# The adapter's transposes and outputs issued between the maxima of the first two units; the value weights in arrays of their own; the first attention loads at the adapter's beginning

## What is computed

```python
qkv = jnp.einsum('btc,oc->bto', x, w_attn)
q, k, v = jnp.split(qkv, 3, axis=-1)          # then 32 heads of 16, q and k rotated
scores = jnp.einsum('bhqd,bhkd->bhqk', q, k) / jnp.sqrt(hd)
attn = jax.nn.softmax(jnp.where(causal, scores, -jnp.inf), axis=-1)
y = jnp.einsum('bhqk,bhkd->bhqd', attn, v)
...
aqkv = jnp.einsum('btc,oc->bto', adapter_wte[None], w_attn)
_, ak, av = jnp.split(aqkv, 3, axis=-1)
ascores = jnp.einsum('bhqd,xhkd->bhqk', q, ak) / jnp.sqrt(C)
ascores = gating[0] * jax.nn.softmax(ascores, axis=-1)
y = y + jnp.einsum('bhqk,xhkd->bhqd', ascores, av)
return jnp.einsum('btc,oc->bto', y, w_proj)
```

## Time and profile before

| | us |
|---|---|
| median of three runs | 1001.11 (1001.0 to 1004.68) |
| the profiled execution: its own time | 1001.68 |
| its span, first to last instruction | 1000.0 |
| adapter stage on PE, first score to the last V product | 89.66 to 126.92 |
| the rest of the adapter on PE and the change of stage | 126.92 to 136.93 |
| first maxima, up to the first scores (L911) | 136.93 to 163.87 |

### The profile page before, as it was taken

The page is one execution under the profiler, slowest core; times in us unless marked ns, Lnnn a source line. Parts: engine busy times, 40 slices in busy tenths (PEclk is TensorE's granted clock), DMA queues, the critical chain, the costliest instruction groups (busy, mean ns, idle before and its releaser), DMA issues. The chain is left out here.

```text
span 1000.0 us, 15159 instructions
## 1 busy us (share of the span) xinstructions
PE 914.7 (91%) x5334; PEld 505.8 (51%) x5334; DVE 648.2 (65%) x1151; ACT 519.6 (52%) x1160; POOL 286.4 (29%) x527
## 2 busy tenths in 40 slices
PE   6897989999999998989689799999999889799997
PEld 4575853434444432865366334343444338577766
DVE  5954447877778760874736678787787418454464
ACT  4441322776767666222734147677776652367630
POOL 2666041223223221024247123222223221013200
PEclk9997985999999999987889789999999999899999
DMA  9331061122212110300014401011110010412001
GB/s 325 97 111 63 1 150 29 52 55 54 66 50 64 38 50 1 106 1 0 1 61 126 116 22 41 26 37 39 40 26 3 2 42 1 151 68 72 14 32 53
DMA packets 50029, 57.14 MB, mean 57 GB/s; under 512 B 8928, under 2 KB 39712, under 8 KB 49952
## 3 DMA queue, kind: packets, MB, share of 16 engines
q1 hardware_dynamic: 48320, 55.75, 18.5%
q10 hardware_dynamic: 1632, 0.39, 0.2%
HBM read 43.41 MB, written 12.32 MB: 56 GB/s over the span
## 5 line engine op out<-in xcount | busy, mean ns | idle before, releaser
L1026 DVE TENSOR_REDUCE mx<-psum 128x1 f32<-128x512 f32 (+3 forms) x640 | 370.8, 631 | 116.4 <-PE psum L891 72.3
L886 PE MATMUL psum<-arena_s 96*128 96x512 bf16 (+3 forms) x768 | 228.2, 352 | 10.3 <-PEq L246 5.9
L972 ACT ACTIVATE arena_p<-psum 128x512 f32<-128x512 f32 (+1 forms) x384 | 185.0, 591 | 93.1 <-PE psum L911 61.4
L911 PE MATMUL psum<-arena_s 99*128 99x512 bf16 (+3 forms) x768 | 204.3, 335 | 8.4 <-ACT arena_p L972 3.3
L972 ACT ACTIVATE arena_x<-psum 128x128 f32<-128x128 f32 (+2 forms) x384 | 134.0, 439 | 87.7 <-PE psum L911 64.8
L886 PEld LDWEIGHTS psum<-arena_s 96*128 96x128 bf16 x768 | 71.5, 100 | 125.5 <-DVE mx L1026 70.2
L911 PEld LDWEIGHTS psum<-arena_s 99*128 99x128 bf16 x768 | 66.9, 98 | 100.0 <-ACT arena_p L972 34.0
L1077 POOL TENSOR_SCALAR_AFFINE_SELECT arena_p<-arena_p 128x256 f32<-128x256 f32 x128 | 50.9, 408 | 204.1 <-ACT arena_p L972 204.1
L891 PE MATMUL psum<-maskb,ident_b 128*128 128x128 bf16 (+1 forms) x384 | 97.5, 254 | 0.0
L261 PE MATMUL psum<-x_h,w 128*128 128x512 f32 x224 | 86.5, 449 | 11.6 <-DVE w L497 8.4
L929 PE MATMUL psum<-arena_p,v_grp 128*32 128x512 f32 (+1 forms) x768 | 90.7, 592 | 0.0
(11 more groups left out here) (210 smaller groups left out, 1186.1 us busy)
## 6 DMA issues: line engine op xcount, KB each, us to landing
arena_s<-q_parts SPq DMA_DIRECT2D x32, 192.0 KB, 2.9
arena_s<-k_parts SPq DMA_DIRECT2D x96, 64.0 KB, 2.3
ff_raw<-in_w_in SPq DMA_DIRECT2D x11, 512.0 KB, 3.5
arena_s<-q_parts SPq DMA_DIRECT2D x32, 128.0 KB, 2.9
arena_w<-in_w SPq DMA_DIRECT2D x12, 256.0 KB, 6.5
q_parts<-arena_p SPq DMA_DIRECT2D x24, 128.0 KB
ff_wd_raw<-in_w_down SPq DMA_DIRECT2D x1, 2560.0 KB, 11.5
k_parts<-arena_p SPq DMA_DIRECT2D x18, 128.0 KB
```

Of the source, the lines that this page charges most:

```text
L886: last = pe.matmul(psum[:, bank, width * n:width * n + width], q_st[0:KS, b % NS, 512 * r + P * i:512 * r + P * i + P], k_st[0:KS, g % NK, ...
L911: pe.matmul(psum[:, 2 * (n % 2) + t, o:512], k_st[0:KM, g % NK, at:at + P], q_st[0:KM, u % NS, 512 * r + o:512 * r + 512], start=True, sto ...
L972: act.activation(pr[n % NP_RING][:, t, o:512], psum[:, 2 * (n % 2) + t, o:512], ACT.Exp, scale=scale).then_inc(exp_ready, 1)
L1026: dve.tensor_reduce(mx[:, b % 2, kc, col:col + 4 * len(heads) - 3:4], src, AX, ALU.max)\
```

## The change

Three edits go together.

First, the turns T and the outputs y leave the adapter stage. There remain scores 0, V0, V1, scores 1 and V2 to V7, with ACT's copies of V. In `attention` of the first layer, PE issues T of tile n after entry 5n of the first maxima and y of tile n after entry 5n + 3, in the PSUM banks 0 to 3. ACT copies them there (in the changed kernel L987 and L990), and its `load_max(0)` comes after the sixth tile. The first scores wait until all eight tiles are copied.

Second, the value columns of the weights get arrays of their own, `wv0`, behind the query and key columns in the same part of `arena_s`.

Third, SP issues `load_first` at the adapter's beginning, once the stores of the stage before have landed; it no longer waits for V7.

```diff
-        w0_hl = [at(f"w0_{n}", M_S + 24576 * n, [P, KC, 3 * C], F32R) for n in range(2)]
+        w0_hl = [at(f"w0_{n}", M_S + 24576 * n, [P, KC, 2 * C], F32R) for n in range(2)]
+        wv0_hl = [at(f"wv0_{n}", M_S + 24576 * n + 16384, [P, KC, C], F32R) for n in range(2)]
...
-    order = [("scores", 0), ("V", 0), ("V", 1), ("scores", 1)]
...
+    order = [("scores", 0), ("V", 0), ("V", 1), ("scores", 1)] + [("V", n) for n in range(2, NT)]
...
         def _(sp):
-
-            sp.wait_ge(turn_ready, turns.index(("V", NT - 1)) + 1)
             stacked.wait_stored(sp)
             stacked.load_first(sp)
...
+                if ad and n == 0:
+                    pe.wait_ge(turn_taken, NT)
+                    pe.wait_ge(y_copied, NT)
...
-            maxima(0, 0)
+            def adapter_turn(n):
+
+                if n >= 2:
+                    pe.wait_ge(turn_taken, n - 1)
+                for t in range(KC):
+                    last = pe.transpose(psum[0:AW, n % 2, P * t:P * t + P],
...
+            def adapter_values(n):
+
+                pe.wait_ge(turn_taken, n + 1)
+                if n >= 2:
+                    pe.wait_ge(y_copied, n - 1)
+                for t in range(KC):
+                    last = pe.matmul(psum[:, 2 + n % 2, P * t:P * t + P], ad["pT"][:, n % 2, t, :],
...
+            for e in range(issued_by(0, 0)):
+                b = next(x for x in range(NU + 1) if issued < first_entry[x + 1])
+                entry(issued, b, lists[b][issued - first_entry[b]])
+                issued += 1
+                tile, step = divmod(e, 5)
+                if ad and tile < NT and step == 0:
+                    adapter_turn(tile)
+                if ad and tile < NT and step == 3:
+                    adapter_values(tile)
...
-            load_max(0)
+            for n in range(NT if ad else 0):
+                act.wait_ge(turn_ready, n + 1)
...
+                act.wait_ge(y_ready, n + 1)
+                act.copy(ad["y"][:, n, :], psum[:, 2 + n % 2, :]).then_inc(y_copied, 1)
+                if n == NT - 3:
+                    load_max(0)
```

More of the change, by code:

```diff
@@ L189, in build @@
             arena_f=arena_f, ident=ident, ident_b=ident_b, maskb=maskb, psum=psum, v_grp=v_grp,
-            w_hl=w0_hl, x_hl=x0_hl, q_parts=q_parts[0], k_parts=k_parts[0], ones=ones, eps=eps,
+            w_hl=w0_hl, wv_hl=wv0_hl, x_hl=x0_hl, q_parts=q_parts[0], k_parts=k_parts[0], ones=ones, eps=eps,
             small_loads=[
@@ L199, in build @@
         wo = [view(arena_f, 8192 * n, [KC, C]) for n in range(2)]
-        adapter(nc, d, ad, x_loaded, x_tok, v_tok, w0_hl, x0_hl, arena_o, ident, gating, psum, stacked,
+        adapter(nc, d, ad, x_loaded, x_tok, v_tok, wv0_hl, x0_hl, arena_o, ident, gating, psum, stacked,
                 wo[0], wo_hl[0])
         attention(nc, 0, att, stacked, arena_o, arena_p, arena_x, v_tok, v_grp, ident_b, maskb, psum,
-                  (x_tok[:, :, :], d["x"].rearrange("(t p) c -> p t c", p=P), x_loaded))
+                  (x_tok[:, :, :], d["x"].rearrange("(t p) c -> p t c", p=P), x_loaded), ad, ident)
         w1_raw = view(v_tok[:, :, :].rearrange("p t c -> p (t c)"), 0, [KC, C + 2 * P])
@@ L317, in cut_of @@
         kind, k, n0 = piece
+        if kind == "w" and n0 == 2 * C:
+            return [w[:, k, n0:n0 + 512], *[a[:, k, :] for a in m["wv_hl"]]]
         return [a[:, k, n0:n0 + 512] for a in ((x_raw, xh, xl) if kind == "x" else (w, wh, wl))]
@@ L565, in _, with adapter @@
                     .then_inc(res_ready, 1)
-def adapter(nc, d, ad, x_loaded, x_tok, v_tok, w_hl, x_hl, arena_o, ident, gating, psum, stacked,
+def adapter(nc, d, ad, x_loaded, x_tok, v_tok, wv_hl, x_hl, arena_o, ident, gating, psum, stacked,
             wo_raw, wo_hl):
@@ L577, in adapter @@
     prob = [view(arena_o, 16384 + 5120 * n, [HT, H * ADP]) for n in range(2)]
-    pT = view(arena_o, 16384 + 10240, [2, KC, P], parts=AW)
-    mx, y_ad = ad["mx"], ad["y"]
-    order = [("scores", 0), ("V", 0), ("V", 1), ("scores", 1)]
[L583 to L591, removed]
+    mx = ad["mx"]
+    ad["prob"] = prob
+    ad["pT"] = view(arena_o, 16384 + 10240, [2, KC, P], parts=AW)
+    order = [("scores", 0), ("V", 0), ("V", 1), ("scores", 1)] + [("V", n) for n in range(2, NT)]
     def heads(a):
@@ L599, in adapter @@
                                                     ("scores_ready", "shifted", "exped", "prob_ready"))
-        turn_ready, turn_taken, y_ready, y_copied = (ph.sem(n) for n in
-                                                     ("turn_ready", "turn_taken", "y_ready", "y_copied"))
+        turn_ready, turn_taken = ph.sem("turn_ready"), ph.sem("turn_taken")
         chain_s = ph.sem("chain")
@@ L628, in _ @@
                     continue
[L629 to L651, removed]
+                if n >= 2:
+                    pe.wait_ge(turn_taken, n - 1)
+                products(pe, psum[:, 4 + n % 2, :],
+                         [lambda k, a=a: a[:, k, P * n:P * n + P] for a in x_hl],
+                         [lambda k, a=a: a[:, k, :] for a in wv_hl]).then_inc(turn_ready, 1)
         @block.scalar
@@ L655, in _ @@
             for what, n in order:
[L656 to L671, removed]
+                if what == "V":
+                    act.wait_ge(turn_ready, n + 1)
+                    if n == 2:
+                        stacked.wait_stored(act)
+                    act.copy(v_tok[:, n, :], psum[:, 4 + n % 2, :]).then_inc(turn_taken, 1)
                 if what == "V" and n in (0, 2):
@@ L761, in attention @@
 def attention(nc, layer, phase, stacked, arena_o, arena_p, arena_x, v_tok, v_grp, ident_b, maskb,
-              psum, x_load=None):
+              psum, x_load=None, ad=None, ident=None):
     q_st, k_st, q_loaded, k_loaded, kr = stacked.q, stacked.k, stacked.q_loaded, stacked.k_loaded, stacked.kr
@@ L837, in attention @@
         o_copied, vg_ready = ph.sem("o_copied"), ph.sem("vg_ready")
+        if ad:
+            turn_ready, turn_taken, y_ready, y_copied = (ph.sem(n) for n in
+                                                         ("turn_ready", "turn_taken", "y_ready", "y_copied"))
         block = ph.block()
@@ L942, in maxima @@
                     issued += 1
-            maxima(0, 0)
+            def adapter_turn(n):
+                if n >= 2:
+                    pe.wait_ge(turn_taken, n - 1)
+                for t in range(KC):
+                    last = pe.transpose(psum[0:AW, n % 2, P * t:P * t + P],
+                                        ad["prob"][n // (NT // 2)][:, n % (NT // 2), AW * t:AW * t + AW],
+                                        ident[:, :])
+                last.then_inc(turn_ready, 1)
+            def adapter_values(n):
+                pe.wait_ge(turn_taken, n + 1)
+                if n >= 2:
+                    pe.wait_ge(y_copied, n - 1)
+                for t in range(KC):
+                    last = pe.matmul(psum[:, 2 + n % 2, P * t:P * t + P], ad["pT"][:, n % 2, t, :],
+                                     ad["av_bd"][:, t, :], start=True, stop=True)
+                last.then_inc(y_ready, 1)
+            for e in range(issued_by(0, 0)):
[7 more added lines that the diff above has]
+                    adapter_values(tile)
             for u, kt in blocks[0:2]:
@@ L984, in load_max @@
                     .then_inc(max_loaded[u % NS], 16)
-            load_max(0)
+            for n in range(NT if ad else 0):
+                act.wait_ge(turn_ready, n + 1)
+                if n >= 2:
+                    act.wait_ge(y_ready, n - 1)
+                act.copy(ad["pT"][:, n % 2, :, :], psum[0:AW, n % 2, :].rearrange(
+                    "p (t q) -> p t q", q=P)).then_inc(turn_taken, 1)
+                act.wait_ge(y_ready, n + 1)
+                act.copy(ad["y"][:, n, :], psum[:, 2 + n % 2, :]).then_inc(y_copied, 1)
+                if n == NT - 3:
+                    load_max(0)
+            if not ad:
+                load_max(0)
             for u in range(NU):
```

## The result

The changed kernel takes 990.54 us (median of 4 runs, 989.28 to 992.53) against 1001.06 of the kernel before: a ratio of 0.9885, interval 0.9856 to 0.9914. Two further sets of runs gave 0.9859 (0.981 to 0.9907) and 0.9869 (0.9834 to 0.9903). It is faster by 1.15 to 1.41% in the three sets, each interval clear of 1; 990.8 was forecast.

What follows compares the result with a forecast made beforehand. PE bounds the adapter until V7, then SP's issues end it; DVE bounds the first maxima. 11.5 us saved less 1.2 gives 10.3: 1001.68 to 991.4, less 0.57 for the median, 990.8; range 987.6 to 995.5.

Steps and rivals of the forecast that it cites:

- The stage's end: Adapter stage: ends 11.5 us earlier, 2.84 from moved turns and outputs, 8.63 from ending with ACT's copy of V7.
- the 8.6 us of tail: Adapter's end: 8.63 us from ACT's copy of V7 to SP's last issue, removable only with early loads.
- Hidden behind DVE at full clock: First maxima: at 2.4 GHz PE's entries, T and y need 21.7 us, below DVE's 24.8, so they cost nothing.
- The sum's 2.5 of 2.7 us for five entries: First maxima: per five entries with their T and y, PE needs 2.5 us against DVE's 2.7.
- Friction and spells: First maxima: DVE waits behind unit 0's T plus zero to two low-clock spells, 0 to 4.2 us together, taken as 1.2.
- priced `load_max(0)` at nothing: First maxima: its 1.34 us issue on ACT delays T6's copy, needed by y6 only 1.6 us later; cost nothing.
- The price set on a spell: First maxima: 3.4 us at low clock would lose 1.5 us, five entries taking PE 4.8 against DVE's 2.7.
- The first scores: Behind the first maxima: the same program as before, only shifted, with no gain of its own.
- the third rival: First scores: full clock lasts into them, giving up to 2.5 us more, 987.1 with no friction; chance 0.10.
- The slow rivals: First maxima: low clock throughout, 1003.5 us, chance 0.05; low clock for half, 996.6 us, chance 0.11.
- One sign of being wrong: Start of the attention: the forecast is wrong if POOL's memsets start later than 126 us.

Runs made afterwards that it cites:

- the last experiment: Changed kernel with V products ahead of the scores and two of POOL's three memsets moved into the adapter stage: 987.52 us, ratio 0.9841 to the kernel before.

## Why the prediction was right

**The stage's end**, 11.5 us, came out at 11.84, 12.31 and 12.35 in the three profiles of the changed kernel. Its two sources are as told: the moved turns, and the loads without which the 8.6 us of tail would have stayed. The runs with one half each show it: 0.3 us for the loads alone, a ratio of 0.9988 for the turns alone. Of the excess, 0.13 is the change of stage itself, 0.46 us behind ACT where it was 0.59 behind SP; the rest lies ahead of V7's end, where the stage took 34.19 us in the first profile and not 37.26 - 2.84 = 34.42.

**Hidden behind DVE at full clock.** DVE is busy 25.02 of 27.73 us, and PE's work lies beside it. The sum's 2.5 of 2.7 us for five entries was rather too low. It took a pair from the old stage at 1.24; between the entries a T takes 0.43 to 0.47 us from start to start and a y 0.89 to 1.00, so the eight pairs need 11.0 us and not 9.9. That still fits beside DVE, but there is little room left: with y doubled, 6.5 of 7 us came into the open.

**Friction and spells**, 1.2 us, measured 0.8, the same in all three profiles, all of it friction. There was no spell, and one premise for it was off: PE waits 1.08 us at the stage's end and 0.51 at the T, not about as long as before (1.67 and 1.76). Nor is the friction only where the prediction put it, behind the empty ring at the T (0.57). Of the 0.79 us, DVE's own busy time is 0.24, and the longest wait, 0.62, is that behind y6. The prediction priced `load_max(0)` at nothing, since y6 needs T6's copy only three entries later; the copy came too late for that, and y6 waits 0.29 or 0.30 for it in all three profiles. The price set on a spell, 1.5 us for 3.4, gives 2.0 for the 4.6 us of low clock in the run with late loads. Measured are 1.6, or 2.1 when the 0.55 are added that T's wait for POOL costs in the changed kernel.

**The first scores**, taken as merely shifted, are 1.7 us shorter in all three profiles, since the clock is still at 1.00. That was the third rival, with a chance of 0.10, and here a step failed: the argument against it took the fall at 144.5 as what entries at DVE's pace bring about. The changed kernel has nine such entries at the end, and the first scores begin behind them at ACT's pace. Half-microsecond windows, two from these entries and one from the first scores:

```profile
152.50:153.00 0.50, 0.23 (x4) 0.08 (x3) 0.50 (x2) 0.00 (x0) 0.00 (x0) 1.00 0.00 0
155.00:155.50 0.50, 0.30 (x3) 0.04 (x1) 0.50 (x2) 0.00 (x0) 0.00 (x1) 1.00 0.00 0
157.00:157.50 0.50, 0.35 (x2) 0.10 (x1) 0.00 (x0) 0.50 (x2) 0.26 (x1) 1.00 0.00 0
```

Some 3 us at that pace, with work ahead of them, don't bring it down here; in the kernel before, the fall followed on a wait of 1.67 us and a spell at low clock. The rival's gain of up to 2.5 was near the 1.7 found. But this gain is not certain. With the same entries at the end the clock stayed at 1.00 through this stretch in the three profiles of the changed kernel and in that with V ahead of the scores. It fell 2.5 to 3.4 us into the first scores in three others: with late loads (16.54 us), with each output twice (16.53) and with the memsets moved (15.27). Why it falls in some and not in others stays open.

**The sum** of these parts is 11.8 - 0.8 + 1.7 = 12.7 us, not 10.3. That the median of the first set fell on the forecast is partly luck: its profiled execution lost 2.85 us in the projection, and of the other runs no trace tells. The second and third set, 13.7 and 12.8 us by their medians, stand nearer to the sum of the parts. The forecast was about 2.4 us too cautious: 1.7 in the first scores, 0.4 in the friction and 0.3 in the stage's end.

**The slow rivals** did not come about. Low clock over the maxima would have needed work between the entries that doesn't hold the clock, and both kinds hold it. The first scores did not wait for `load_max(0)`. It and POOL were not quite out of the way: y6 waits for the one, and T's 0.51 for the other is worth the 0.55 us that the last experiment gains.

**The signs.** One sign of being wrong came true by the letter: POOL's memsets start at 127.75 in the first profile, later than 126 (126.16 and 123.44 in the others). The times named there assumed that the adapter begins at 89.66. From the adapter's first score the memsets start at 127.75 - 92.51 = 35.24 us, where it was 136.75 - 89.66 = 47.09, and 36.3 had been allowed. The end of the first loads (102.5 for 102), the first entry (127.94 for 125.4) and the first scores (155.67 for 153.5) are late in the first profile for the same reason.

## What to carry to other kernels

Two engines that end a stage together must both be moved: look for the second last thing behind the one that is removed, and for how long its own queue needs after its release (here 9.2 us of issuing). A stretch that another engine paces is a place for TensorE work, up to what fits between its steps, in pieces shorter than what the buffers ahead hold; it can also keep the clock up for what follows, as in four of seven profiles here. An engine that looks idle can still be late at one place: an issue of 1.34 us in front of a copy was enough. A median that agrees with the forecast does not confirm its parts; compare them stretch by stretch, in more than one execution.

## What the runs showed of the hardware

- Transposes alone, 14 for each five entries, kept the granted clock at 1.00 where entries alone saw it fall to 0.50.
- At the adapter's beginning, behind 5 us without PE work, narrow fp32 scores ran at 0.50 for all of their 7.1 us; 512-column products in their place had the clock up after 3.3.
- While ACT issued one DMA (1.34 us), its next copy did not start: T6's copy begins 0.10 us after the issue ends, 1.20 after its T, where the others begin 0.63 to 0.67 after theirs.
- The same program may see the clock fall in the projection (68 to 76 us) in one execution and not in the next: 0.65 and 0.50 against 1.00 in the windows above, some 3 us of the span.
